# Attention with row halves in separate orders, exps of one tile, V products of eight key tiles, and x spilled to memory

## The reference

```
x = x + 0.5 * ffn(layernorm(x))
x = x + attention(layernorm(x))
x = x + 0.5 * ffn(layernorm(x))

def attention(X):                      # b=1, s=4096, d=256, 16 heads of 16
    ctx = X @ We.T                     # 32 wide
    influence = ctx @ ctx.T
    scores = Q @ K.T * SCALE + 0.1 * influence
    attn = softmax(scores)
    return (attn @ V) @ Wo.T
```

## Time and profile before

| what | value |
|---|---|
| device time, median of 3 runs | 3914.05 us (3909.14 to 3915.34) |
| the profiled execution | 3907.77 us, of which the span is 3906.0 us |
| TensorE busy | 3752.5 us (96%) |
| VectorE busy | 3237.7 us (83%) |
| ScalarE busy | 2529.3 us (65%) |
| GpSimd busy | 1027.2 us (26%) |

### The profile page before, as it was taken

One profiled execution on the slowest core, in us unless ns is written; L12 is line 12 of the kernel. 1 busy time (PEld: TensorE's weight loads), 2 busy tenths in 40 slices (PEclk: granted clock), 3 DMA queues, 4 the chain that ended last, 5 costly groups with the idle time before them and its releaser, 6 DMA issues. The chain is left out here.

```text
span 3906.0 us, 88246 instructions
## 1 busy us (share of the span) xinstructions
PE 3752.5 (96%) x28132; PEld 2149.9 (55%) x28132; DVE 3237.7 (83%) x5240; ACT 2529.3 (65%) x2897; POOL 1027.2 (26%) x779
## 2 busy tenths in 40 slices
PE   3999799999999999999999999999999999999699
PEld 3988355545554555555545554555555555555598
DVE  7996688888888888888888888888888888886698
ACT  4764366666666666666666666666666666667475
POOL 4990111111111111111111111111111111111597
PEclk9999799999999999999999999999999999999899
DMA  3004511212121212121212121212121212111000
GB/s 128 0 0 177 95 39 39 47 39 46 38 47 37 47 38 45 40 47 39 47 40 47 38 47 37 44 38 47 40 45 39 48 39 47 38 47 41 33 19 23
DMA packets 305371, 179.03 MB, mean 46 GB/s; under 512 B 196864, under 2 KB 236192, under 8 KB 304544
## 3 DMA queue, kind: packets, MB, share of 16 engines
q1 hardware_dynamic: 299504, 171.49, 18.9%
q10 hardware_dynamic: 5552, 3.44, 0.5%
HBM read 140.35 MB, written 29.36 MB: 43 GB/s over the span
## 5 line engine op out<-in xcount | busy, mean ns | idle before, releaser
L1333 DVE TENSOR_REDUCE tops<-coarse 128x1 f32<-128x512 f32 x4069 | 2632.0, 686 | 505.7 <-PE coarse L1179 402.6
L1315 ACT ACTIVATE probs<-fine 128x1024 f32<-128x1024 f32 x2048 | 1985.3, 1021 | 1008.7 <-PE fine L1214 1005.6
L1225 PE MATMUL o_ps<-probs,vh 128*32 128x512 f32 x8192 | 1093.0, 606 | 0.3 <-ACT probs L1315 0.3
L1200 PE MATMUL fine<-query_a,key_a 64*128 64x512 f32 x4096 | 921.1, 446 | 20.3 <-issue 14.5
L1200 PEld LDWEIGHTS fine<-query_a,key_a 64*128 64x128 f32 x4096 | 387.5, 185 | 926.7 <-ACT probs L1315 849.6
L1179 PE MATMUL coarse<-key_a,max_query 64*128 64x512 f32 x4069 | 829.7, 401 | 20.3 <-DMA max_query<-scratch_c_query 15.5
L1214 PE MATMUL fine<-query_b,key_b 33*128 33x512 f32 x4096 | 817.4, 394 | 0.0
L1206 PE MATMUL fine<-query_c,key_c 64*128 64x512 f32 x4096 | 814.2, 393 | 0.0
L939 POOL TENSOR_TENSOR ot<-ot 49x512 f32<-49x512 f32 x127 | 162.4, 1279 | 2155.7 <-ACT ot L1291 2155.7
L1179 PEld LDWEIGHTS coarse<-key_a,max_query 64*128 64x128 f32 x4069 | 387.1, 186 | 136.6 <-DVE tops L1333 66.7
L1214 PEld LDWEIGHTS fine<-query_b,key_b 33*128 33x128 f32 x4096 | 389.2, 185 | 84.0 <-DMA query_b<-neg_max 0.3
(11 more groups left out here) (188 smaller groups left out, 2602.7 us busy)
## 6 DMA issues: line engine op xcount, KB each, us to landing
query_c<-scratch_c_query SPq DMA_DIRECT2D x256, 128.0 KB, 2.6
query_a<-scratch_q_hi SPq DMA_DIRECT2D x512, 32.0 KB, 1.8
query_a<-scratch_c_query SPq DMA_DIRECT2D x256, 64.0 KB, 2.0
query_b<-neg_max SPq DMA_DIRECT2D x1024, 0.5 KB, 2.0
max_query<-scratch_q_hi SPq DMA_DIRECT2D x508, 32.0 KB, 1.8
max_query<-scratch_c_query SPq DMA_DIRECT2D x254, 64.0 KB, 1.9
query_b<-scratch_q_lo SPq DMA_DIRECT2D x256, 32.0 KB, 2.3
x_all<-in_L_attn_X SPq DMA_DIRECT2D x4, 1024.0 KB, 12.4
```

The lines of the kernel that those rows point to most:

```text
L1200: pe.matmul(fine[i % 2][:, r, :], key_a[kp][half_rows(r, 0, HALF), cols], query_a[half][half_rows(r, 0, HALF), :], start=True, stop=False)
L1225: last = pe.matmul(o_ps[32 * j:32 * (j + 1), :], vh[kp][:, kt, :], probs[:, kt // 2 % RING, kt % 2, :], start=g == 0, stop=g == NG - 1)
L1315: act.activation(probs[:, i % RING, :, :], fine[i % 2][:, :, :], ACT.Exp).then_inc(probs_ready, 1)
L1333: dve.tensor_reduce(tops[n][:, idx // KB, idx % KB:idx % KB + 1], bank, AX.X, ALU.max).then_inc(tops_ready, 1)
```

## The change

Six things are changed.

1. **Orders of the row halves.** Two strings, one for each row half, say for each of the 16 waves of a group whether the half makes a coarse product (`C`) or the next of a tile's three fine products (`f`). The kinds are no longer the same in both halves. `GROUP` becomes 4, so a group has 16 waves; eight coarse products in it are waited for and signalled one by one.
2. **Exps of one tile.** ScalarE makes 32 exps of 512 columns in a step, in the order in which tiles end (`TILES_ENDED`), in place of 16 of 1024. A tile's first product waits for the exp four before it.
3. **V products of eight key tiles.** `times_v` runs four times in a step with eight products, two in each set of 32 columns.
4. **probs in x's place.** The ring of probabilities holds 8 pairs (`RING` = 8, two groups) instead of 4, and lies over `x_all`, which the attention does not read.
5. **x is spilled.** The first FFN writes each tile of x to memory when it is done; four transfers bring x back over `v_all` during the last head, and the output phase and the second FFN use it there.
6. **Loops.** The sixteen blocks of a pair of heads are written out; only the loop over pairs of heads stays.

The core of the diff:

```diff
-RING = 4
-GROUP = 2
+RING = 8
+GROUP = 4
...
-SKIP_AFTER = 23
-SUMS_AFTER = 1
+
+WAVES = ["CCfffCfffCffffff", "fffCffffffCfffCC"]
+CHUNKS = 3
...
+GROUP_WAVES, TILES_ENDED = group_of_waves()
+UNITS_IN_GROUP = len(WAVES[0]) * 2 - 2 * GROUP * CHUNKS
+TILES_IN_GROUP = 2 * GROUP
+SUMS_AFTER = TILES_IN_GROUP - 1
...
                     for j in range(2 * GROUP):
-                        kt = 2 * GROUP * g + j
-                        last = pe.matmul(o_ps[32 * j:32 * (j + 1), :], vh[kp][:, kt, :], probs[:, kt // 2 % RING, kt % 2, :], start=g == 0, stop=g == NG - 1)
+                        kt, part = 2 * GROUP * g + j, j % 4
+                        last = pe.matmul(o_ps[32 * part:32 * (part + 1), :], vh[kp][:, kt, :], probs[:, kt // 2 % RING, kt % 2, :],
+                                         start=g == 0 and j < 4, stop=g == NG - 1 and j >= 4)
                     last.then_inc(pv_done, 1)
...
+                    for g in range(NG):
...
+                        for wave in GROUP_WAVES:
+                            for r, tile, what, order in wave:
+                                if tile is None and within(t):
+                                    wait_for_bank(t, n, unit % UNITS + order, UNITS * b + UNITS_IN_GROUP * g + order)
+                                elif tile is not None and what == 0:
+                                    pe.wait_ge(probs_ready, P_LEAD + TILES * s + TILES_IN_GROUP * g + TILES_ENDED.index((tile, r)) + 1 - 2 * FINE)
+                                elif tile is not None and what == CHUNKS - 1 and g == 0 and tile == 0:
+                                    pe.wait_ge(m_loaded[half], M_DMAS // 2 * (s - half) + M_DMAS)
+                            for r, tile, what, order in wave:
+                                if tile is None and within(t):
+                                    place = UNITS * b + UNITS_IN_GROUP * g + order
+                                    coarse_product(coarse[place % COARSE][:, :], n, keys, unit % UNITS // KB, r, what).then_inc(coarse_ready, 1)
+                                elif tile is not None:
+                                    last = score_chunk(half, kp, GROUP * g + tile, r, what)
+                                    if what == CHUNKS - 1:
+                                        last.then_inc(fine_ready, 1)
+                        if g == 0:
                             before(lambda: times_v(s - 1, last_keys, NG - 1))
-                        elif i % GROUP == GROUP - 1:
-                            times_v(s, kp, i // GROUP - 1)
+                        else:
+                            times_v(s, kp, g - 1)
...
+                    for g in range(NG):
+                        act.wait_ge(pv_done, NG * s + g + 1)
+                        for e, (tile, r) in enumerate(TILES_ENDED):
+                            i = GROUP * g + tile
+                            act.wait_ge(fine_ready, TILES * s + TILES_IN_GROUP * g + e + 1)
+                            act.activation(probs[:, i % RING, r, :], fine[i % 2][:, r, :], ACT.Exp).then_inc(probs_ready, 1)
+                            if g == 0 and e == SUMS_AFTER:
...
+                    spilled, x_spilled = x_spill
+                    with sp.Fori(0, TT) as t:
+                        sp.wait_ge(x_done, t + 1)
+                        sp.dma_start(spilled[:, bass.ds(t, 1), :], x_all[:, bass.ds(t, 1), :]).then_inc(x_spilled, 16)
```

More of the change, by code:

```diff
@@ L893, with group_of_waves @@
 AHEAD = 16
-SKIP_AFTER = 23
-SUMS_AFTER = 1
+WAVES = ["CCfffCfffCffffff", "fffCffffffCfffCC"]
+CHUNKS = 3
+def group_of_waves():
+    waves, tiles, products, ended = [], [0, 0], [0, 0], []
+    count = 0
+    for k in range(len(WAVES[0])):
+        wave = []
+        for r in range(2):
+            if WAVES[r][k] == "C":
+                wave.append((r, None, products[r], count))
+                products[r] += 1
+                count += 1
+            else:
+                tile, chunk = divmod(tiles[r], CHUNKS)
+                wave.append((r, tile, chunk, None))
+                tiles[r] += 1
+                if chunk == CHUNKS - 1:
+                    ended.append((tile, r))
+        waves.append(wave)
+    return waves, ended
+GROUP_WAVES, TILES_ENDED = group_of_waves()
+UNITS_IN_GROUP = len(WAVES[0]) * 2 - 2 * GROUP * CHUNKS
+TILES_IN_GROUP = 2 * GROUP
+SUMS_AFTER = TILES_IN_GROUP - 1
 INVERT_AFTER = 7
@@ L1179, in coarse_product, with wait_for_bank @@
                     return pe.matmul(bank, max_query[n][half_rows(r, 0, HALF), q * P:(q + 1) * P],
                                      key_a[keys][half_rows(r, 0, HALF), kb * 512:(kb + 1) * 512], start=True, stop=True)
-                def max_scores(t, n, keys, idx):
+                def wait_for_bank(t, n, idx, place):
                     if idx == 0:
                         pe.wait_ge(mq_loaded[n], MQ_DMAS * ((t - n) // 2 + 1) if isinstance(t, int) else MQ_DMAS // 2 * (t - n) + MQ_DMAS)
[L1186 to L1193, removed]
@@ L1208, in scores_last @@
-                def scores_last(s, half, kp, i):
-                    cols = slice(i * P, (i + 1) * P)
-                    if i == 0:
-                        pe.wait_ge(m_loaded[half], M_DMAS // 2 * (s - half) + M_DMAS)
-                    for r in range(2):
-                        last = pe.matmul(fine[i % 2][:, r, :], key_b[kp][half_rows(r, 0, M_ROW + 1), cols], query_b[half][half_rows(r, 0, M_ROW + 1), :],
-                                         start=False, stop=True)
-                    last.then_inc(fine_ready, 1)
+                    behind = COARSE if place >= PLACES % COARSE else PLACES % COARSE
@@ new lines, in wait_for_bank, with score_chunk @@
+                    pe.wait_ge(tops_ready, UNITS * t + idx - behind + 1)
+                def score_chunk(half, kp, i, r, chunk):
+                    cols = slice(i * P, (i + 1) * P)
+                    keys, query = [(key_a[kp], query_a[half]), (key_c, query_c[half]), (key_b[kp], query_b[half])][chunk]
+                    rows = half_rows(r, 0, HALF if chunk < CHUNKS - 1 else M_ROW + 1)
+                    return pe.matmul(fine[i % 2][:, r, :], keys[rows, cols], query[rows, :], start=chunk == 0, stop=chunk == CHUNKS - 1)
```

144 lines of the change are left out of this document (59 added, 85 removed).

## The result

The changed kernel takes 3858.41 us, median of 4 runs (3853.8 to 3860.08). The kernel before, in the same comparison, takes 3914.7 (3909.14 to 3916.2). The ratio is 0.9857, with a 95% interval of 0.984 to 0.9874. The profiled execution took 3857.52 us, against 3907.77 before. So the change saves about 56 us in the medians, and 50 between the two profiled executions, where 17 were forecast.

What follows compares the result with a forecast made beforehand. TensorE was taken to set the attention's pace. V's −1.49 us a step, less 1.36 for held waves, left −17 us in all, other parts 0: 3914 − 17 = 3897 us; own range 3878 to 3912, overall 3840 to 4000.

Steps and rivals of the forecast that it cites:

- Last fine product to ScalarE: Handoff in the attention: an exp starts 0.51 us after its tile's last fine product starts.
- 5.78 us of work, held to 6.05: One group of 16 waves and four V rounds: 5.78 us unheld, 0.27 us held, 6.05 us in all.
- V products of eight tiles: TensorE's V products in the attention: four switches fewer in a step, −1.49 us a step, −191 us in all.
- Held waves: TensorE's waves waiting for maxima or exps in the new order: 1.36 us a step of V's gain goes to them.
- VectorE to a held wave: Handoff in the attention: a held wave starts effectively 0.17 us after the end of the maximum it waits for.
- ScalarE to a held wave: Handoff from an exp's end to a held wave: no row showed it, so VectorE's 0.17 us was taken.
- Exps of 512 columns: ScalarE's smaller exps in the attention: 0.595 us each, 0.49 us from start to start by overlap.
- rival 1: ScalarE's exps don't overlap and follow 0.60 us apart: +111 us, 4025 us; chance 0.15.
- The later copies: Sums copied later: total about 1.6 us later, SyncE's queue keeps 0.4 us idle a step; cost nothing.
- Rival 4: SyncE's queue sets the step, its 0.4 us of slack gone: +0.3 us a step, 3935 us; chance 0.03.
- the gain is used up: V's rounds cost 0.46 us or each attention handoff 0.03 more: 3912 to 3928 us; chance 0.25.
- the waits are hidden: Row halves don't hold each other, or handoffs are shorter: 3723 us, 3840 if a third is hidden; chance 0.12.

Runs made afterwards that it cites:

- Experiment 1: Changed kernel with one more, long-met wait ahead of each exp, its value computed after the wait for the scores; 3897.25 us, ratio 0.995.
- experiment 4: Changed kernel with V's eight products in two runs of four, after wave 7 and after wave 15 of each group; 3997.42 us, ratio 1.0207.
- experiment 3: Changed kernel without ScalarE's two copies of the sums in steps 0 to 126, so the output is not attention's; 3824.75 us, ratio 0.977.
- experiment 5: Changed kernel with one wave order for both row halves, exps of one tile kept; 4046.25 us, ratio 1.0341.
- experiment 6: Changed kernel with one order for both halves and exps of 1024 columns; count raised by 2 (first form) 4104.56 us, by 1 (second form) 4071.12 us.
- experiment 2: Kernel before the change, with ScalarE waiting for the V products first and the scores second; 3916.69 us, ratio 1.0001.

## Why the prediction was right or wrong

**The sign and the mechanism were right, the gain was three times as large as forecast.** The failed step is the list of handoffs, in which three terms were mis-sized. "Last fine product to ScalarE ... 0.51 us" measures 0.43. I read it from a row of the kernel before as if it were a property of the engines. It was one of the program: 0.08 of it was the sequencer's arithmetic for another wait, which the changed kernel does not have ahead of its exps. The exps' spacing, 0.49, measures 0.48. The maxima's, 0.61, measures 0.598 for queued ones, which the kernel before hardly had. Because "5.78 us of work, held to 6.05" is a small difference of large numbers, these three are 38 us together, by the walk 16, 6 and 16: the 0.012 of the maxima weighs as much as the 0.08 of the exps' start. Experiment 1 puts the first two back and gets 39 us back, but only 24 of them in the step: the match with the whole miss is chance, and 24 of 39 is what it shows. That the third, the maxima, is the remaining 0.10 us a step (24.48 forecast, 24.38 in experiment 1) rests on the walk alone; no run changed it by itself.

**By its steps:**
- *V products of eight tiles*, −1.49 us a step. The rounds come at 0.454, 0.429, 0.429 and then 0.542 us to the next wave: confirmed, and experiment 4 gives the price of the four switches from the other side.
- *Held waves*, +1.36. Measured 24.19 − 23.12 = 1.07. Wave 5 is held 0.13 as forecast, wave 7 after the copies 0.25 as forecast (experiment 3 takes away 0.27). Waves 10 to 15: 0.06, where 0.13 was forecast.
- *VectorE to a held wave*, 0.17, and *ScalarE to a held wave*, assumed 0.17: right. Waves held by a maximum start 0.16 to 0.17 us after its end in the changed kernel, and waves held by an exp of 512 columns 0.16 after it in experiment 5. After an exp of 1024 columns it is 0.22 to 0.23 (experiment 6).
- *Exps of 512 columns* take 0.595 and don't wait for each other's end, unlike the copies. That settles rival 1, and the estimate by the Trainium skill (ScalarE: Activation LUTs, "What ACT_TABLE_LOAD costs") of 0.61 and 0.52 us was too long by 0.04 in the spacing; the walk by it had no gain.
- *The later copies*, 0. In the total, nothing is lost, but my 0.4 us of idle queue was wrong. SyncE's queue, by its timeline:

```profile
2031.44 0.37 SPq L1025 DMA_DIRECT2D max_query<-scratch_c_query  x1
2033.75 0.78 SPq L1024 DMA_DIRECT2D query_a<-scratch_q_hi  x2
2046.37 0.59 SPq L951 DMA_DIRECT2D few<-total  x1
```

  At the end of its step it idles from 2031.81 to 2033.75, 1.9 us, as much as in the earlier trace rows. The load of `few` does come 12.6 us after that of `query_a` where it came 11.2, but no step waits for the queue: TensorE's steps are at the walk's length. Rival 4 is out.
- *Spill and return of x*, 0: the windows above show TensorE at the same pace in the first FFN with x going out. The return of x was not tried by itself.
- *Loops*, 0: the outer return costs 3.9 us on average (V's runs there are 8.7 to 10.6 us apart against 6.0), about as before, but six times and not seven. Over 1 us of it goes with the lower clock: the one return without it costs 2.8 us. That the inner loops' end gives nothing was not tried by itself; the rest of the kernel is 3 us longer, not shorter.

**The rivals.** 2, "the gain is used up", asked for handoffs 0.03 longer; they were 0.08 shorter, the same leverage with the other sign. 3, "the waits are hidden", named shorter handoffs as one of its ways, and that is the way in which it came a fifth true: held time fell from 1.36 to 1.07. Its other way, halves that don't hold each other, is refuted: from 600 to 3400 us of the changed kernel the two products of a wave never start more than 0.06 us apart, held or not. Experiment 5 also comes out at 25.67 for 25.65 and experiment 4 at 25.28 for 25.2, both by a walk in which each half holds the other.

## What to carry to other kernels

When a change makes a loop of several engines tight, its gain is set by handoffs of some tenths of a microsecond, and these have to be read together with what the waiting engine's sequencer does between the wait and the work: put the wait that is met last directly ahead of the instruction, and compute the values of other waits before it. A value computed ahead of the exps cost nothing in one kernel (experiment 2) and, ahead of every exp, 0.6% in the steps of another (experiment 1), so such an edit is worth trying again after each change of order. And when a difference of two large sums is forecast, say what 0.01 us in each handoff is worth before giving a range: here, by the walk, it was 2 us for the scores' handoff, 6 for the exps' spacing and 14 for the maxima's. When a total moves by more than the step explains, look at the granted clock of the places where the loop returns.

## What the runs showed of the hardware

- An ACTIVATE that finds ScalarE idle starts about 40 ns after the recorded end of the matmul that it waits for when its wait is the last thing before it (33 to 45 in the changed kernel and experiments 2 and 5; 67 to 70 in experiment 6's second form, for which I have no reason). It starts mostly 115 to 124 ns after when its sequencer still computes a value (one instruction of 35 ns; the kernel before, experiment 1), and 125 to 131 when the wait is an instruction of its own (experiment 6, first form).
- Exps of 512 columns that never wait follow each other by 0.477 us (0.494 behind one that found the engine idle) while their recorded length grows from 0.59 to 0.66. So the length of a queued one is not its price. With a value computed between them they are 0.494 apart on average.
- Copies of 49x512 out of one PSUM bank don't overlap (0.60 apart for a length of 0.59), and one of 113 rows takes the same 0.60 as one of 49.
- A maximum of 128x512 that finds VectorE idle lasts 0.69 us, and the next follows by 0.608; a queued one mostly lasts 0.68, and the next follows by 0.598. Where maxima come in pairs, as before and in experiments 5 and 6, the first spacing is the rule.
- ScalarE's table is loaded in each of the seven passes of the outer loop, 1.28 us, though only exps and copies run there. Held back behind the data (experiment 1) it costs about 0.5 us a return, an estimate from one return at the same clock.
- TensorE's granted clock can fall to its lower level in or just behind a pause of about 3 us at the loop's return, for 0 to 10.2 us, and not alike in all returns of one run: V's runs there are 8.7 us apart without it, 9.7 to 10.6 with 3.4 us of it, 11.4 to 12.1 with 6.8 (changed kernel, experiment 1).
- After an exp of 512 columns a held wave starts 0.16 us after its end, after one of 1024 columns 0.22 to 0.23 (experiments 5 and 6).
